# Six input tiles and three weight shares quantized in other batches, and a new order for the end of a cross-attention and feed-forward kernel

## The reference

```
x = x + xattn(layernorm(x), ctx, ctx)              # softmax(q k^T / sqrt(32)) v, then Wo
def fp4_quant_dequant(x):                          # blocks of 16 along the last axis
    scale = max(max|x| / 6, 1e-12)                 # one for each block
    q = GRID[searchsorted(MID, |x / scale|)] * sign(x) * scale
def fp4_linear(x, w): return fp4(x) @ fp4(w).T
n = layernorm(x)
x = x + fp4_linear(silu(fp4_linear(n, w_gate)) * fp4_linear(n, w_up), w_down)
```

## Time and profile before

| | us |
|---|---|
| time, median of 3 runs (lowest, highest) | 2138.82 (2137.6, 2141.08) |
| the profiled execution: its time, its span | 2137.12, 2135.3 |
| PE, DVE, ACT busy of the span | 2070.8 (97%), 1708.5 (80%), 863.6 (40%) |
| mean granted clock of PE | 0.987 |

### The profile page before, as it was taken

The page is one execution under the profiler, slowest core; times in us unless marked ns, Lnnn a source line. Parts: engine busy times, 40 slices in busy tenths (PEclk is TensorE's granted clock), DMA queues, the critical chain, the costliest instruction groups (busy, mean ns, idle before and its releaser), DMA issues. The chain is left out here.

```text
span 2135.3 us, 42263 instructions
## 1 busy us (share of the span) xinstructions
PE 2070.8 (97%) x16730; PEld 1785.7 (84%) x16730; DVE 1708.5 (80%) x2859; ACT 863.6 (40%) x1753; POOL 144.7 (7%) x162
## 2 busy tenths in 40 slices
PE   6999999999999999999999999978899999999998
PEld 5888888888988888888888898856688888888886
DVE  6777777777777777777768777777999999999985
ACT  5555455455554555555545455453111111111111
POOL 0000000000000000000000000001101001001000
PEclk9999999999999999999999999979899999999999
DMA  4443444534445344344553545454343343344331
GB/s 162 119 137 98 130 110 135 140 97 132 109 133 139 101 126 139 100 137 109 132 139 95 132 109 134 111 151 129 107 133 109 113 137 112 114 131 113 114 113 38
DMA packets 159462, 257.36 MB, mean 121 GB/s; under 512 B 34096, under 2 KB 102704, under 8 KB 156832
## 3 DMA queue, kind: packets, MB, share of 16 engines
q1 hardware_dynamic: 158544, 253.34, 43.1%
q10 hardware_dynamic: 720, 1.31, 0.2%
HBM read 109.88 MB, written 57.54 MB: 78 GB/s over the span
## 5 line engine op out<-in xcount | busy, mean ns | idle before, releaser
L756 DVE TENSOR_REDUCE row_max<-gate_bank 128x1 f32<-128x376 f32 (+1 forms) x576 | 301.8, 536 | 114.6 <-PE gate_bank L565 113.6
L539 PE MATMUL proj_bank<-attention_operands 128*128 128x256 f32 x2304 | 304.8, 282 | 0.0
L517 PE MATMUL proj_bank<-attention_operands 128*128 128x376 f32 (+1 forms) x1536 | 288.8, 337 | 3.6 <-ACT attention_operands L690 3.1
L539 PEld LDWEIGHTS proj_bank<-attention_operands 128*128 128x128 f32 x2304 | 288.8, 189 | 0.4 <-DVE q_part L786 0.2
L654 ACT ACTIVATE probs<-score_bank 125x448 f32<-125x448 f32 x384 | 208.0, 542 | 163.5 <-PE score_bank L579 161.1
L517 PEld LDWEIGHTS proj_bank<-attention_operands 128*128 128x128 f32 x1536 | 262.1, 190 | 5.9 <-issue 3.4
L1402 ACT ACTIVATE f_act_gate<-gate_bank 128x512 f32<-128x512 f32 (+1 forms) x84 | 47.3, 564 | 528.4 <-PE up_bank L1342 528.4
L654 ACT ACTIVATE probs<-up_bank 125x448 f32<-125x448 f32 x384 | 208.0, 542 | 126.7 <-PE up_bank L579 124.2
L1342 PE MATMUL gate_bank<-gate_up,early 128*128 128x512 f32 (+1 forms) x984 | 226.7, 380 | 17.2 <-DVE early L1484 9.3
L1342 PEld LDWEIGHTS gate_bank<-gate_up,early 128*128 128x128 f32 x984 | 183.7, 191 | 50.2 <-DVE early L1484 9.6
L1342 PE MATMUL up_bank<-gate_up,early 128*128 128x512 f32 (+1 forms) x984 | 223.8, 376 | 0.0
(11 more groups left out here) (146 smaller groups left out, 3194.5 us busy)
## 6 DMA issues: line engine op xcount, KB each, us to landing
kstack<-k_low SPq DMA_DIRECT2D x256, 93.8 KB, 2.3
kstack<-early SPq DMA_DIRECT2D x256, 93.8 KB, 2.2
kstack<-k_high SPq DMA_DIRECT2D x256, 93.8 KB, 2.2
strips_scratch<-f_strips SPq DMA_DIRECT2D x25, 960.0 KB, 3.7
f_turned<-strips_scratch SPq DMA_DIRECT2D x100, 240.0 KB, 4.4
ctx_raw<-in_ctx SPq DMA_DIRECT2D x15, 1500.0 KB, 8.0
qstack<-early SPq DMA_DIRECT2D x384, 28.0 KB, 1.9
qstack<-q_part SPq DMA_DIRECT2D x384, 28.0 KB, 1.8
```

Source lines behind the costliest of these rows:

```text
L517: last = nc.tensor.matmul(out[:, 0:hi - lo], w_hi_lo[W_K][ws][:, c, g * P:(g + 1) * P], ctx_part[cs][:, c, lo:hi], start=(n == 0), stop=(n ...
L539: last = nc.tensor.matmul(out[:, 0:256], ctx_part[cs][:, c, kt * KW:kt * KW + P], w_hi_lo[W_V][ws][:, c, half * 256:(half + 1) * 256], sta ...
L756: nc.vector.tensor_reduce(row_max[:, m, kh:kh + 1], mbank[:, 0:KSPLIT[kh + 1] - KSPLIT[kh]], AX.X, ALU.max).then_inc(max_reduced, 1)
```

## The change

1. Six x tiles (`AHEAD`), 0 to 5, are normed, quantized, block-transposed and stored to DRAM during batches 6 to 12, one per batch: loaded and normed in slot 2, eight steps in slot 3, the last in slot 0 of the next batch (`AHEAD_UNITS`). Tiles 0 and 1 come back turned by DMA in slot 0 of the last batch, without the turns on PE; tiles 2 to 5 come back so in the feed-forward (`x_ahead`).
2. The three weight shares of the last batch move to slot 2 of batches 12, 13 and 14, with new places there. The load of the next batch's x in slot 0 moves from place 2.6 to 7.0.
3. The last batch's slots 2 and 3 and the end units get a list of their own (`LAST`), in which all 22 weight tiles, the maxima of group 3, and the gate products stand; these are cut in halves of six matrix products, two of them in slot 3.
4. In the feed-forward the quantization of tiles 1 to 3 has hidden rows only, that of tile 0 is gone; tile 3's first gate and up product stands in tile 2's list, ahead of the first down product.

```diff
-SLOT_TILES = 16
+SHIFTED = 2
...
+AHEAD = 6
+AHEAD_BATCH = 6
...
-FFN_SLOTS = (0, 1, 3)
-PROJECTIONS = ("k", "q", "v", "xt", "out", "first_turn")
+BATCHES = 16
+FFN_SLOTS = [(b, g) for b in range(BATCHES - 1) for g in range(4) if g != 2 or b >= BATCHES - 4]
...
-        "ffn_quant": (5.33, 7.73, 8.21, 8.66, 9.42, 9.43, 9.88, 11.15, 11.15),
+        "ffn_quant": (3.84, 4.49, 4.93, 5.92, 7.04, 7.22, 9.26, 10.46, 11.22),
...
+AHEAD_UNITS = {
+    (0, 2): [(6.2, ("ahead_load",)), (10.5, ("ahead_norm",)), (11.3, ("ahead_norm2",))],
+    (0, 3): [(0.8, ("ahead_quant", 1)), (2.3, ("ahead_quant", 2)), (2.7, ("ahead_quant", 3)), (3.8, ("ahead_quant", 4)),
+             (10.4, ("ahead_quant", 5)), (10.7, ("ahead_quant", 6)), (11.2, ("ahead_quant", 7)), (11.5, ("ahead_quant", 8))],
+    (1, 0): [(2.1, ("ahead_quant", 9)), (3.0, ("ahead_square",)), (3.5, ("ahead_store",))],
+}
...
+        if not (last and g == 2):
+            add(at["max"], *[("max", g + 1, n) for n in range(2 * MT)])
+            add(at["shift"], ("shift", g + 1, 0))
...
+    for (later, slot), placed_units in AHEAD_UNITS.items():
+        tile = b - AHEAD_BATCH - later
+        if slot == g and 0 <= tile < AHEAD:
+            for place, unit in placed_units:
+                add(place, (unit[0], tile, *unit[1:]))
     if g == 0 and not last:
-        add((at["load"],) * 2, ("load_ctx", 1), ("load_x", 1))
+        add((at["load"], 7.0), ("load_ctx", 1), ("load_x", 1))
...
+LAST = {
+    "max": (0.22, 0.93, 1.64, 2.9, 3.08, 3.77, 4.48, 5.19, 5.68, 6.35, 7.32, 7.44, 8.34, 9.45),
+    "shift": 10.3,
+    "tiles": ((0.48, 0.63), (3.34, 4.35), (5.94, 6.84), (8.47, 10.74), (10.76, 10.92), (11.35, 11.58), (11.79, 14.61), (12.49, 15.18), (14.58, 15.76), (16.49, 18.15), (19.05, 20.08), (20.16, 22.47), (22.92, 23.29), (23.07, 23.89), (23.98, 24.48), (24.05, 25.3), (24.36, 27.08), (25.14, 27.27), (25.36, 27.61), (27.05, 31.27), (27.62, 31.98), (31.78, 32.03)),
+    "x": ((7.96, 9.93), (14.89, 15.38)),
+    "gates": (15.05, 22.79, 25.79, 26.51, 29.0, 29.23, 31.79, 32.47),
+}
...
+    placed = [(-23.4, ("first_load", 0)), (-23.4, ("first_load", 1))]
+    placed += [(-3.0, ("turn_load", j)) for j in range(RAWS)]
+    for j, (hi, lo) in enumerate(LAST["tiles"]):
+        placed += [(hi, ("turn_hi", j)), (lo, ("turn_lo", j))]
...
+            placed.append((lo + 0.1, ("turn_load" if j > 4 else "turn_load_early", j + RAWS)))
+    for t, (hi, lo) in enumerate(LAST["x"]):
+        placed += [(hi, ("first_turn_hi", t)), (lo, ("first_turn_lo", t))]
+    placed += [(at, ("max", 3, n)) for n, at in enumerate(LAST["max"])] + [(LAST["shift"], ("shift", 3, 0))]
+    placed += [(at, ("first_gate", n // 4, n // 2 % 2, n % 2)) for n, at in enumerate(LAST["gates"])]
+    placed += [(12.0 + at, unit) for at, unit in attend_units(NG - 1) if at >= 12]
+    placed += [(26.0, ("inverse", 3, 0)), (26.1, ("inverse", 3, 1)), (26.2, ("heads", 3)), (26.3, ("heads_hi", 3)),
+               (26.4, ("sum_lo", 3)), (28.0, ("out", 0, 0)), (29.0, ("out", 0, 1)),
+               (30.0, ("store_x1", 0, 0)), (30.0, ("store_x1", 0, 1))]
...
+                    m, half = u[2], u[3]
+                    pe.wait_ge(turn_lo, 4 * (2 * t + m + 1))
+                    pe.wait_ge(max_reduced, 2 * MT * NG * batches)
+                    pe.wait_ge(shift_copied, NG * batches)
+                    if t == 1 and m == 1:
                         pe.wait_ge(exp_done, 12 * NG * batches)
...
+                    steps = [(c, xs_, ws) for c in range(KC) for xs_, ws in PASSES]
+                    for n in range(6 * half, 6 * half + 6):
...
+                elif kind == "ahead_load":
+                    sp.wait_ge(made["xt"], 2 * (b + 2))
+                    sp.wait_ge(x1_stored, 32 * ((P * t + P - 1) // SQ + 1))
+                    sp.dma_start(xn_whole[:, 0, :], x1.rearrange("b s d -> (b s) d").rearrange("(n p) d -> n p d", p=P)[
...
+    with_h, with_x = tile > 0, tile + 2 >= AHEAD and left > 2
+    event = with_h or with_x
...
+    hidden_at = {0: 0, 1: 4, 2: 4, 3: 6}.get(tile, 8)
+    shifted = tile == SHIFTED
...
+    return [*([] if tile == SHIFTED + 1 else [("gate_up", n, 0)]),
+            *([("hidden", n, 0), ("gate_up", n, 1), ("hidden", n, 1)] if hidden_at == 0 else []),
+            *quant_and_hidden(1, 2, 3, 4, 5, 6), *fresh(3, ("norm", n + 3)),
+            *quant_and_hidden(7), *when(-3, ("store", n - 3)), *when(-1, ("load_res", n - 1)), *fresh(4, ("load", n + 4)),
+            *when(-2, ("h_hi", n - 2)), *when(1, *([("x_hi", n + 1)] if tile > 0 else [])), *quant_and_hidden(8),
+            *fresh(3, ("normalize", n + 3)), *quant(9), *when(-2, ("h_lo", n - 2)),
+            *([("gate_up", n, 1), ("hidden", n, 1)] if hidden_at else []), ("gate_up", n, 2),
+            *strips, *when(1, *([("x_lo", n + 1)] if tile > 0 else [])), *([("x_ahead", n + 2)] if 0 < tile < AHEAD - 2 else []),
+            *([("hidden", n, 2), ("gate_up", n + 1, 0)] if shifted else []),
+            *when(-2, *[("down", n - 2, c) for c in range(3)]), *([] if shifted else [("hidden", n, 2)]), *bounce]
...
-    units = [("load", 2), ("load", 3)] + [("late_load", k) for k in range(LATE_RAWS)]
+    units = [("x_ahead", 2)] + [("late_load", k) for k in range(LATE_RAWS)]
...
+                elif kind == "x_ahead":
+                    sp.wait_ge(x_lo, tile)
```

More of the change, by code:

```diff
@@ L173, in attend_units, with slot_units @@
     return [(place, (kind, g, p)) for kind, places in (("pv", "pv"),) for p, place in enumerate(at[places])]
-def slot_units(g, first, last):
+def slot_units(g, b):
+    first, last = b == 0, b == BATCHES - 1
+    here = b * NG + g
+    share_slots = [NG * n + slot for n, slot in FFN_SLOTS]
     at = PLACES[g]
@@ L202, in slot_units @@
         add(at["sum_lo"], ("sum_lo", g - 1))
[L203 to L212, removed]
+    for chain, slot in enumerate(share_slots):
+        if slot == here:
+            add(at["ffn_quant"], *[("ffn_quant", chain, n + 1) for n in range(QSTEPS)])
+            add(at["ffn_quant"][-1] + 0.02, ("ffn_square", chain))
+        if slot + 1 == here:
+            add(0.2, ("ffn_store", chain))
+            add(6.0, ("ffn_regroup", chain))
+        if slot - 1 == here:
+            add(0.3, ("ffn_load", chain))
     if g == 1 and not first:
@@ L299, with attention @@
 LAST_UNITS = last_units()
[L300 to L305, removed]
+END_UNITS = [unit for _, unit in sorted(LAST_UNITS[NG], key=lambda item: item[0])]
+def attention(nc, ctx, dram, ident, ln_consts, x1, x_ahead, ffn_raw, ffn_quant, ffn_squares, batches, region, ctx_raw, early, gate_up, xqt, first_banks, fs):
     def sb(name, shape, dt=F32):
@@ L1086, in quantize_step, with period_units @@
     return dve.tensor_tensor(blocks(out), blocks(t), spread(scale), ALU.mult)
[L1089 removed]
+def period_units(tile, n, left):
+    with_h, with_x = tile > 0, tile + 2 >= AHEAD and left > 2
+    event = with_h or with_x
     def has(k):
[L1097 removed]
+        return tile + k >= 0 and k < left
     def quant(*steps):
[L1100 removed]
+        return [("quant", n, s, with_h, with_x) for s in steps if event]
@@ new lines, in fresh @@
+    def fresh(k, *units):
+        return list(units) if tile + k >= AHEAD and k < left else []
+    strips = [("strips", n, with_h, with_x)] if event else []
+    bounce = [("bounce", n, with_h, with_x)] if event else []
+    hidden_at = {0: 0, 1: 4, 2: 4, 3: 6}.get(tile, 8)
+    shifted = tile == SHIFTED
+    def quant_and_hidden(*steps):
+        return [u for s in steps for u in quant(s) + ([("hidden", n, 0)] if s == hidden_at else [])]
+    return [*([] if tile == SHIFTED + 1 else [("gate_up", n, 0)]),
[8 more added lines that the diff above has]
+            *when(-2, *[("down", n - 2, c) for c in range(3)]), *([] if shifted else [("hidden", n, 2)]), *bounce]
@@ L1235, in phases @@
             i, n = (0, tile) if tile < 3 else ((tile - 1) // 2, 1 + (tile - 1) % 2)
-            units = period_units(n, first=tile, left=tiles - tile)
-            if tile == 0:
-                units = [u for u in units if u[0] not in ("x_hi", "x_lo")]
+            units = period_units(tile, n, tiles - tile)
             body(i, with_late(units, late[tile]) if tile < 2 else units)
```

264 lines of the change are left out of this document (116 added, 148 removed).

## The result

| | before | changed |
|---|---|---|
| median of 4 runs each (lowest, highest), us | 2139.58 (2137.6, 2141.08) | 2162.51 (2158.41, 2166.01) |
| profiled execution's span, us | 2135.3 | 2156.6 |
| PE, DVE, ACT busy, us | 2070.8, 1708.5, 863.6 | 2080.1, 1710.1, 864.1 |

The ratio is 1.0106 (95%: 1.0094 to 1.0118): slower by 1.1%, where 2120.5 and faster were forecast, and outside the range.

A forecast was written before the change was run, and what follows sets the result against it. It took PE to bound the attention and later feed-forward, with DVE holding PE between them. 2137.1 - 11 (last batch) - 14 (feed-forward start) + 5.2 (norm) + 1.2 (x steps) + 2 (shares) = 2120.5 us; range 2107 to 2131.

The forecast's parts named there:

- the hole: Last batch's slot 2 to the feed-forward's first tiles, 1397.1 to 1521.8: DVE holds PE; at most some 50 us to gain.
- both gains: Last batch's slots 2, 3 and end units gain 11 us (0 to 21); feed-forward start gains 14 (8 to 19).
- the last part: Signs to look for: last batch's slot 2 under 20 us, first feed-forward wait 3, tile 2's x_lo wait under 5.
- x tiles in batches 6 to 12: Seven us of DVE a tile: steps cost 1.2 us together (0 to 6), stalls at the norm 5.2 (0 to 42).
- all beside PE's 87.2: Middle batches: the x tiles' DVE work runs alongside PE's 87.2 us a batch, where DVE has 20 us to spare.
- stacking ends about 3 us before its score needs it, which covers that: Batches 12 to 14: SP's added store, load and regroupings for moved shares are covered; the shares cost 2 us together (0 to 6).
- the norm behind the x tile's load: Slot 2, batches 6 to 11: DVE's norm awaits the load (L = 3.3 us) ahead of the shift product, costing 5.2 us.
- The x steps and the shares' steps on DVE: Middle batches: x tiles' quantizing steps cost 1.2 us together (0 to 6), three moved shares 2 together (0 to 6).
- C: Rival, slower: DVE stands at the norm for a late x tile in all six batches; 2157 at L = 9.6; chance 0.07.
- middle batches of 90 and more throughout: Sign that the forecast is wrong; it expected 87.2 to 88 us, and 89 to 90.5 in batches 10 and 11.
- A: Rival: the middle is nearly free (cost 2 us) and the two gains are 13 and 16; 2110; chance 0.24.
- B: Rival: something else holds the last batch's slow stretch, so gains are smaller; 2129.5, or 2135.5; chance 0.19.

The follow-up runs named there:

- the best kernel: The kernel with three edits, with tile 3's first gate and up product put back behind the first down product: 2115.48 us, 0.9893 of before.
- the kernel with three edits: Changed kernel with x store first and x load behind slot 1's low stack, norm behind the shift product, regroupings in next slot 1: 2119.30 us, 0.9909.

## Why the prediction was wrong

**Right: the bound, the hole and both gains.** Slots 2, 3 and the end units gave 12.3 us (forecast 11), the feed-forward start 12.1 (forecast 14). Slot 2 is under 20 us, the first feed-forward wait is 3.05, that for tile 2's `x_lo` 3.91, all as the last part said. The first down product is 155 us behind the last batch's start (1395.0), inside 148 to 158 (by the sum 152). The split was a little off: slot 2 gave 9.2 us (8.1 counted), slot 3 2.6 (0.7), the end units 0.5 (2.2). In the feed-forward the term that was too small is the clock. Tile 2's three products took 17.9 us behind their wait and tile 3's first 7.2, where 15.5 and 5.6 were counted: 4.0 more, where 1 was taken off for all waits. The wait at tile 3's product was forecast at 2.4 and measured 2.60. That pulling this product ahead costs 4.3 us against leaving it was not seen.

**The step that failed: the moved load of x.** Under "x tiles in batches 6 to 12", "all beside PE's 87.2" priced DVE's steps and the norm, and listed for SP only what stood ahead of the x tile's load. The diff also moves `load_x` from 2.6 to 7.0 and adds a wait for the tile's store; neither was given a price. Behind the wait stand slot 1's stacking and the share's store, behind these `k_low` and `fw_square` on DVE, behind them PE. It cost about 22 us: slot 1 falls from 30.9 to 16.9 when the store goes first, and to 8.5 when the load also goes behind the stack (3.8 of these 22.4 are in batch 14, whose figure varies). The trace of before showed how much room there was: `k_low` already waited for this stack, 0.52 us in batch 7 and 2.84 in batch 12, whose slot 1 is the one of 26.7 us in place of 26.1.

**The second: "stacking ends about 3 us before its score needs it, which covers that".** The low stack has an earlier customer than the score, the `k_low` that overwrites its source. A regrouping more cost 6.5 us in batch 14 of the changed kernel's trace, and 2.2 to 4.8 in others with the same regroupings, where 2 were counted for three shares in all. Moving the regroupings, and nothing else, removed it.

**Right in kind, too small: the norm behind the x tile's load.** Forecast 5.2 us from L = 3.3. Moving the norm took slot 3 from 11.5 to 0.6, so it cost about 11. The waits at the first score add up to 8.1 us: L was 4.0 (the landing of `xn<-x_scratch` above) in place of 3.3, and the tile was issued up to 1.2 us later in its slot than the sum had it (batch 8), though 1.0 and 1.8 us earlier in batches 9 and 10. The other 3.4 are what the slots of batches 8 and 11 lost beyond their waits, at a clock of 0.93, and the sum has no term for that. SP's stand at `load_x` is not the reason: with it gone, slot 3 still loses 12.3.

**The x steps and the shares' steps on DVE.** With the x steps narrowed on the best kernel no difference can be told (1.2 counted), and slot 2, where the shares' steps went, adds nothing in batches 12 to 14. This part is right for that kernel. In the changed kernel narrowing gave some 8 us by the ratio; why it did is open.

**The rivals.** C had the sign, and DVE standing at the norm, but its price of 42 us hung on a landing time of 9.6 us that did not come (L was 4.0). The greater part of the price came from SP's order. The sign "middle batches of 90 and more throughout" came for batches 7 to 11 and 14 only. A, the free middle, fell; B fell, since both gains came. The total of the kernel with three edits, 2119.3, lies near the 2120.5 forecast, but that is luck: it is not the kernel that was forecast, and it lacks the norm's wait, for which 5.2 were counted.

**Open.** Why moving the norm also shortened slot 1 by the 6.5 us outside batch 14; what the last 7.4 us of the middle are (5.0 of it in slot 1); why narrower steps helped only in the changed kernel.

## What to carry to other kernels

An engine that issues in order passes every wait on to all that stands behind it: for each wait that a change adds to a DMA queue, list what is queued behind it and who waits for that, before pricing the wait itself; a stand of 3.5 to 5 us in each of six batches, ahead of the low stack, was the most of 22 us, and right behind the stack it cost nothing that the total shows. The entry that hurts need not be the next one: here the share's store, 16 us of stacking further down, cost PE more than the stack. A buffer's copy has two customers, the reader of the copy and the next writer of the source, and the writer may be the earlier one. A product pulled ahead of another helps only if its inputs are ready first.

## What the runs showed of the hardware

A store of 256 KB issued 0.5 us behind a load of 1500 KB took 7.3 us to land (median of five), and 2.8 us when it was issued first: a small transfer behind a large one on the same queue pays for a good part of it. The Trainium skill ("DMA: Bandwidth & Descriptors", section "Queues, rings and completion order") says that each DMA engine takes the descriptors of a ring in order; with the 436 GB/s of its section "Anatomy of one DMA", which is written for GpSimd's path, the context ahead is an estimated 3.5 us, which on top of 2.8 makes 6.3. The trace agrees in kind and measured more, 7.3.

A wait of PE can cost clock besides its own length. In the changed kernel's feed-forward twelve gate products of 512 columns took 5.29 us behind a wait of 3.91 us, 4.24 behind one of 2.60, and 3.03 behind one of 0.35. The granted clock was 0.52 in the first stretch (1522.3 to 1527.4), near the lower of the two levels of 1.2 and 2.4 GHz, and 1.00 in the third. In the attention, waits of 2.06 and 2.86 us were followed by a loss of another 1.6 us each, waits of 1.21 and 1.48 us by none. The length of the wait does not settle it alone: behind the wait of 3.05 us at 1498.04 the clock stayed at 1.00.
